# Attention 0: the values of both query blocks of a tile in one visit behind the second block's query step

## What is computed

```python
q = jnp.einsum('bqd,hd->bqh', x, wq).reshape(B, Qlen, N_HEADS, HEAD_DIM)
...
scores = jnp.einsum('bhqd,bhkd->bhqk', q, k) / np.sqrt(HEAD_DIM).astype(np.float32)
attn = jax.nn.softmax(scores.astype(jnp.float32), axis=-1).astype(q.dtype)
out = jnp.einsum('bhqk,bhkd->bhqd', attn, v)
```

## Time and profile before

| | us |
|---|---|
| median of 3 runs | 1646.51 |
| lowest and highest run | 1643.49, 1650.69 |
| span of the profiled execution | 1646.7 |
| PE busy in it | 1468.3 (89%) |
| DVE, ACT, POOL busy | 1020.8, 756.4, 476.8 |

### The profile page before, as it was taken

How to read it: one execution, slowest core, us unless ns; L and a number is a source line. 1 busy time by engine, 2 the same in 40 slices (tenths; PEclk the granted TensorE clock), 3 DMA queues, 4 the chain that set the end, 5 groups by cost and what they waited for, 6 DMA issues and landing times. The chain is left out here.

```text
span 1646.7 us, 30889 instructions
## 1 busy us (share of the span) xinstructions
PE 1468.3 (89%) x11198; PEld 1181.4 (72%) x11206; DVE 1020.8 (62%) x1607; ACT 756.4 (46%) x1941; POOL 476.8 (29%) x491
## 2 busy tenths in 40 slices
PE   6999779999999999978999939999779999996377
PEld 5999778888888888746887728888556666664133
DVE  3223437767767777544233228777457999997794
ACT  2222117767757767753112102122057777774343
POOL 1111001000010110000011003323368888885155
PEclk9999989999999999998999969999899999999688
DMA  7332246536535535546545342200032222220022
GB/s 243 123 127 99 80 80 149 134 85 148 138 83 139 140 83 135 132 143 223 179 154 179 115 153 77 77 26 13 20 79 64 70 65 64 58 58 1 0 102 102
DMA packets 136844, 170.51 MB, mean 104 GB/s; under 512 B 31110, under 2 KB 109256, under 8 KB 136728
## 3 DMA queue, kind: packets, MB, share of 16 engines
q1 hardware_dynamic: 136728, 168.93, 36.5%
HBM read 85.36 MB, written 33.19 MB: 72 GB/s over the span
## 5 line engine op out<-in xcount | busy, mean ns | idle before, releaser
L1142 ACT ACTIVATE a_prob<-a_psS,a_negmax 128x256 f32<-128x256 f32 x512 | 237.3, 484 | 157.1 <-DVE a_negmax L1065 157.0
L1065 DVE TENSOR_REDUCE a_negmax<-a_psS 128x4 f32<-128x1024 f32 x128 | 154.3, 1206 | 69.3 <-PE a_psS L958 67.2
L887 POOL COPY a_recip<-a_recip_head 128x256 f32<-128x256 f32 x64 | 25.6, 400 | 503.6 <-DVE a_recip_head L1110 503.6
L968 PE MATMUL a_psT<-ident,a_prob 128*128 128x128 f32 x1024 | 137.2, 278 | 14.4 <-issue 6.1
L933 PE MATMUL a_psQ<-a_xT_hi,wq_hi 128*128 128x256 f32 x456 | 135.4, 297 | 0.4
L968 PEld LDWEIGHTS a_psT<-ident,a_prob 128*128 128x128 f32 x1024 | 115.9, 143 | 23.5 <-issue 12.5
L1159 ACT COPY a_probT<-a_psT 128x512 f32<-128x512 f32 x208 | 115.9, 610 | 34.0 <-PE a_psT L968 33.3
L933 PE MATMUL a_psQ<-a_xT_lo,wq_hi 128*128 128x256 f32 x456 | 127.7, 280 | 0.0
L933 PE MATMUL a_psQ<-a_xT_hi,wq_lo 128*128 128x256 f32 x456 | 127.5, 280 | 0.0
L1142 ACT ACTIVATION_READ_ACCUMULATOR a_prob<-a_psS,a_negmax 128x1 f32 x512 | 109.4, 214 | 0.0
L1317 PE MATMUL p_psY<-p_w_hi,p_o_hi 128*128 128x512 f32 x256 | 104.3, 407 | 2.7 <-DVE p_o_lo L1345 2.7
(11 more groups left out here) (242 smaller groups left out, 3684.3 us busy)
## 6 DMA issues: line engine op xcount, KB each, us to landing
a_q_stack<-a_q_hi SPq DMA_DIRECT2D x128, 128.0 KB, 2.6
a_q_stack<-a_q_lo SPq DMA_DIRECT2D x128, 128.0 KB, 2.8
c_nat<-in_ctx SPq DMA_DIRECT2D x8, 1024.0 KB, 5.4
rows<-in_x SPq DMA_DIRECT2D x8, 1024.0 KB, 5.8
scratch_o<-a_oT SPq DMA_DIRECT2D x64, 128.0 KB, 2.1
p_o_lo<-scratch_o SPq DMA_DIRECT2D x8, 1024.0 KB, 5.6
p_x<-in_x SPq DMA_DIRECT2D x8, 1024.0 KB, 7.6
scratch_x<-p_x SPq DMA_DIRECT2D x8, 1024.0 KB, 4.0
```

What stands on the lines that cost most here:

```text
L887: nc.gpsimd.tensor_copy(recip[:, t % 2], recip_head[:, t % 2].unsqueeze(3).broadcast_to([P, TT, JH0, HD0])).then_inc(recip_ready, 1)
L968: last = nc.tensor.transpose(psT[:, kt, j * P:(j + 1) * P], prob[:, n % 2, j, kt * P:(kt + 1) * P], ident[:, :])
L1065: nc.vector.tensor_reduce(negmax[:, n % 2, :], psS[:, bank:bank + 2, :].rearrange("p a (j k) -> p (a j) k", k=S), AX_X, ALU.max, negate=Tr ...
L1142: last = nc.scalar.activation(prob[:, n % 2, j, :], psS[:, 2 * (n % 2) + j // 2, (j % 2) * S:(j % 2 + 1) * S], ACT.Exp, bias=negmax[:, n % ...
```

## The change

`values` takes a tile t in place of a unit n and does both blocks, 16 instructions in place of twice 8, and then the transposes of the reciprocals. It is called once in each odd step, behind the query step; before, it was called in each step between the scores and the query step, one unit late. The probabilities of the second block are thus used in the step that transposes them, behind a wait for their copies. The buffers and the other engines' programs stay as they are.

```diff
-            def values(b, u, n):
-                t, qb = n // TT, n % TT
-                if qb == 0:
-                    pe.wait_ge(o_ready, KT * b + t + 1)
+            def values(b, u, t):
+                pe.wait_ge(o_ready, KT * b + t + 1)
                 for kt in range(TT):
-                    pe.wait_ge(psT_copied[kt], UNITS * b + n + 2)
-                for kt in range(TT):
-                    for j in range(JH0):
-                        head = (t // REP0) * JH0 + j
-                        nc.tensor.matmul(psO[j * HD0:(j + 1) * HD0, 0, qb * P:(qb + 1) * P],
-                                         v0[:, u, kt, head * HD0:(head + 1) * HD0], probT[:, n % 2, kt, j, :],
-                                         start=(kt == 0), stop=(kt == TT - 1))
-                if qb == TT - 1:
-                    pe.wait_ge(recip_ready, KT * b + t + 1)
-                    ...
+                    pe.wait_ge(psT_copied[kt], UNITS * b + TT * t + TT + 1)
+                for qb in range(TT):
+                    for kt in range(TT):
+                        for j in range(JH0):
+                            head = (t // REP0) * JH0 + j
+                            nc.tensor.matmul(psO[j * HD0:(j + 1) * HD0, 0, qb * P:(qb + 1) * P],
+                                             v0[:, u, kt, head * HD0:(head + 1) * HD0], probT[:, qb, kt, j, :],
+                                             start=(kt == 0), stop=(kt == TT - 1))
+                pe.wait_ge(recip_ready, KT * b + t + 1)
+                ...
@@ body of the PE's loop
-                        if n:
-                            values(b, u, n - 1)
                         if more:
                             query_step(b + 1, 1 - u, n)
                         else:
                             for quarter, kt in update_steps.get(n, ()):
                                 update_part(quarter, kt)
-                    values(b, u, UNITS - 1)
+                        if n % TT == TT - 1:
+                            values(b, u, n // TT)
```

More of the change, by code:

```diff
@@ L970, in transposes @@
                     last.then_inc(psT_full[kt], 1)
-            def values(b, u, n):
-                t, qb = n // TT, n % TT
-                if qb == 0:
-                    pe.wait_ge(o_ready, KT * b + t + 1)
+            def values(b, u, t):
+                pe.wait_ge(o_ready, KT * b + t + 1)
                 for kt in range(TT):
-                    pe.wait_ge(psT_copied[kt], UNITS * b + n + 2)
-                for kt in range(TT):
-                    for j in range(JH0):
-                        head = (t // REP0) * JH0 + j
-                        nc.tensor.matmul(psO[j * HD0:(j + 1) * HD0, 0, qb * P:(qb + 1) * P],
-                                         v0[:, u, kt, head * HD0:(head + 1) * HD0], probT[:, n % 2, kt, j, :],
-                                         start=(kt == 0), stop=(kt == TT - 1))
-                if qb == TT - 1:
-                    pe.wait_ge(recip_ready, KT * b + t + 1)
[L986 to L989, removed]
+                    pe.wait_ge(psT_copied[kt], UNITS * b + TT * t + TT + 1)
[7 more added lines that the diff above has]
+                pe.wait_ge(recip_ready, KT * b + t + 1)
+                for s in range(TT):
+                    last = nc.tensor.transpose(psO[:, 1, s * P:(s + 1) * P],
+                                               recip[:, t % 2, s, :, :].rearrange("p j c -> p (j c)"), ident[:, :])
+                last.then_inc(psO_full, 1)
             for f in range(XFILLS):
```

## The result

| | before | after |
|---|---|---|
| median | 1645.24 us (4 runs) | 1669.44 us (4 runs) |
| ratio to before | 1 | 1.0148, 95% interval 1.0134 to 1.0161 |
| span of the profiled execution | 1646.7 us | 1668.2 us |
| PE busy in it | 1468.3 us | 1449.7 us |

The change makes the kernel 24 us slower, and PE does the same 11,200 matmuls in 19 us less. Slower was forecast, but by 43 us, and 1669.4 lies under the range (1671 to 1709).

A forecast was written before the change was run, and what follows sets the result against it. PE was taken to set the pace of attention 0, with DVE and ACT close behind in the light part. The terms 19.4 + 15.4 + 4 + 4.3 = 43 us on 1646.7 gave 1690 us, range 1671 to 1709.

The forecast's parts named there:

- Part 1: Steps 0 to 3 in 7 batches: PE waits for DVE's split and ACT's copies, 2.8 us a batch, 19.4 us.
- part 3: PE's block prices change with their neighbours in the 42 heavy pairs: 4 us slower, bounds 0 and 8.
- Part 2: Queries of steps 7 and 13 wait for DVE's chain with norm work, 1.23 and 1.34 us each: 15.4 us.
- Part 4: Last batch: ACT's chain in light pairs 2.2 us, values now behind the a_update waits 2.1 us; 4.3 us.
- V V: Two blocks of values back to back on PE, priced 1.16 us; clearly under 1.1 us would make the prediction wrong.
- (b): On PE, fewer changes of kind win: 64 visits saved give 13 us, the kernel gets faster, 1630 us; chance 0.03.
- (c): PE's clock falls too, behind the waits of 15 light or norm-laden stretches: +24 us, 1714 us; chance 0.11.
- (a): DVE and ACT run ahead enough that no new wait appears on PE: 1646 to 1654, 1650 us; chance 0.04.
- (d): Waits in the light pairs and at the norm steps come out at half: 1672 us; chance 0.09.

The follow-up runs named there:

- e5: Kernel after, with DVE's statistics and normalising one step later and normalise_o behind the split of the next odd step; 1649.85 us, 1.0032 of before.
- e2: Kernel after, with DVE's statistics of step 6 and normalising of step 12 issued one step later, behind the split; 1654.27 us, 1.0047 of before.
- e3: Kernel after, with the one visit per tile moved to the next even step, between scores and query, and three probT units; 1641.84 us, 0.9971 of before.
- e1: Kernel before, with each unit's values in two visits in batches 0 to 6, the second half behind the query step; 1694.69 us, 1.0289 of before.
- e8: Kernel after, with the update matmuls of the last batch 128 columns of the array wide instead of 40; 1673.66 us in a single run.
- e6: e3 with DVE's statistics and normalising one step later and normalise_o moved behind the split of the next odd step; 1629.99 us, 0.9911 of before.
- e7: Kernel after, with two visits in the odd step, first block between scores and query step, second behind the query step; 1667.79 us, 1.0136 of before.

## Why the forecast was wrong

**Part 1 (light pairs, 19.4 us): right in its chains.** In steps 2 and 3 the chain of DVE came out at 4.14 us and that of ACT at 5.06, the pair at 7.13 us instead of 7.37. Of these 0.24 us, 0.15 are the two blocks of values, whose price belongs to part 3. e5 shows that ACT's chain is the one that ends last.

**Part 2 (norm work in steps 6 and 12, 15.4 us): right.** 4.79 us for 4.80, and e2 gave some 16 us back.

**Part 4 (last batch, 4.3 us): right.** From the scores of its step 0 to the end of the stage the last batch grew from 57.33 us (677.44 to 734.77) to 62.74 (699.74 to 762.48), by 5.4 us. The updates wait 2.3 us more (5.9 for 3.6), the values wait 3.2 and 2.9 us for the copies in the two light pairs, and one stretch more is at half the clock.

Parts 1, 2 and 4 are waits, and together they said 39.1 us. PE's idle time in the stage grew by 41.7, a near match of two measures that aren't quite the same (see above).

**Part 3 (changes of kind, +4 us with bounds 0 and 8): this is the step that failed.** It priced V straight behind V at the 0.58 of V before R, and took the query at 1.50 us in any place but before values. PE's busy time in the stage fell by 14.2 us instead of rising by 4: an error of 18 us, which is the miss (43 forecast, 27.5 in the stage, 24 in the medians). Four terms make it up, each read from steps 8 and 9 above (T, S, V, R and Q are the letters of the prediction): V V 1.01 for 1.16 us (0.15 x 64 = 10 us); a query between scores and transposes 1.37 for 1.50 (0.13 x 42 = 5); one between scores and values 342.98 - 341.47 = 1.51 for 1.61 (0.10 x 42 = 4); and scores before a query at the low bound 0.55, not in the middle (4). Of these 23 us the clock took some 5 back: PE was busy 23.0 us of the stage at 0.50 of full speed, against 12.8 in before, and half of the 10 us is lost.

The sum closes better than it should. The four terms leave out that the scores and fillers of the light pairs got cheaper too, and that busy time counts scores ahead of a wait at 0.72 us and not 0.55, in 31 waits more; by an estimate from the rows (28 scores at 0.1 and 14 fillers at 0.14 us; 31 waits at 0.17) each is worth some 5 us, and they have opposite signs. In a pair where nothing waits the terms hold alone: steps 8 and 9 take 6.86 us, where 7.23 + 0.10 was forecast, and the difference of 0.47 is what the prices of this pair add up to (0.15 + 0.13 + 0.10 + 0.10). A whole batch, from the scores of step 0 to those of the next step 0, went from 61.1 to 64.5 us (batch 5), and not to 66 or 67.

The rows of before held the warning: 1.50 us was only ever read behind reciprocals or values, so it had the cost of leaving them in it, and the sum used it for a query that no longer follows them. It counted the other side of the same border, R at 0.27 before transposes where it was 0.18 before a query, and so charged the move without what the move gave back. The forecast's bound for V V allowed for most of it (-7 of the -10 us), and its own sign of being wrong, V V clearly under 1.1 us, is met; but the bounds of the query were never opened below. Its bounds themselves are off by a microsecond: 43 less 4 and 7 is 32 and not 31.

**The rivals.** (b) was wrong in its sign and right in its rule: its 13 us from fewer visits were 14 in after and 18 in e3 by busy time. The Trainium skill, TensorEngine Tiling (Array Packing), Key Properties, says that changing the tiling mode drains TensorE; e1, e3 and e8 agree that a change of width costs, with 0.2 to 0.3 us for a visit of 32-column products between 128-column ones. What it did not decide is the total: the chain of 4.14 us that it needed under 2.4 did not move. (c), the clock, allowed 24 us on top and gave some 5: of the 15 stretches with waits that it named, three at most were followed by 3.4 us at 0.50 of full speed (648.64, 713.50 and 740.80 above), not all of them. At such a stretch its price was right: from the scores of step 3 to those of step 4 batch 6 takes 652.32 - 645.39 = 6.93 us, where batch 1 takes 320.12 - 314.77 = 5.35. (a) and (d) fell with the chains, which came out whole. The mechanisms that decide were seen; the prices of the blocks were carried over from neighbours that no longer stood next to them.

## What to carry to other kernels

When a block moves on the engine that sets the pace, list every neighbour pair that the move makes or breaks, and price each block by its neighbours, for a price read start to start holds part of what the block before it left behind. Then ask which cross-engine hand-over the moved block was standing in front of; the sum of both is the answer, and either alone has the wrong size here. Batching the visits was a gain of 14 to 18 us and the place of the visit a loss of 42, and one more buffer slot for the probabilities, with DVE's norm work and normalise_o one step later (e6), keeps the first without the second (0.9911 of before).

## What the runs showed of the hardware

A visit of PE to 32-column products between 128-column ones costs 0.2 to 0.3 us of PE's busy time beyond its rows, measured three times: e1 adds 98 visits to before (+30.9 us busy, of which 4 for the reciprocals and some 4 for the clock; 0.23 us), e3 takes 64 from before (-17.9 us, at the same clock; 0.28 us), e7 adds 64 to after (+11.9 us, some 16 with the clock taken out; 0.25 us). By the rows about 0.14 us lie inside the visit and up to 0.1 us in each neighbour, and the neighbours differ from place to place. The block ahead pays by the width of what follows: scores take 0.65 us before 32 or 40 columns and 0.55 us before 128, with the product otherwise the same. The block behind pays too: transposes take 0.85 us behind an update block of 40 columns and 0.79 behind the same block at 128.
